# Score banks kept apart from query banks, and a planner that enters subtractions one by one

## What is computed

```python
xn = x / jnp.maximum(l2, 1e-12) * scale_norm * gamma
q, k, v = (qkv[:, :, 0], qkv[:, :, 1], qkv[:, :, 2])
sim = jnp.einsum('bihd,bjhd->bhij', q * scale_attn, k)
sim = jnp.where(causal_mask, neg, sim)
attn = jax.nn.softmax(sim, axis=-1)
out = jnp.einsum('bhij,bjhd->bihd', attn, v)
```

## Time and profile before

| | us |
|---|---|
| median of three runs | 1998.93 |
| the profiled execution, its own time | 2002.52 |
| its span in the profile | 2000.7 |
| big-head stage, from its first matmul to its last | 880.85 to about 1409.2 |

### The profile page before, as it was taken

One profiled execution on the slowest core, in us unless ns is written; L12 is line 12 of the kernel. 1 busy time (PEld: TensorE's weight loads), 2 busy tenths in 40 slices (PEclk: granted clock), 3 DMA queues, 4 the chain that ended last, 5 costly groups with the idle time before them and its releaser, 6 DMA issues. The chain is left out here.

```text
span 2000.7 us, 40527 instructions
## 1 busy us (share of the span) xinstructions
PE 1787.3 (89%) x15880; PEld 958.9 (48%) x15880; DVE 1559.0 (78%) x2275; ACT 1374.9 (69%) x2569; POOL 419.6 (21%) x650
## 2 busy tenths in 40 slices
PE   6799999999999888849999999899679999998785
PEld 2122222222222278826888888789312322233384
DVE  5899999999999443547988788877578979785434
ACT  3499999999999743426665666566347998888331
POOL 4201000000000403343432221312320011122413
PEclk8599999999999988969999999999868999999597
DMA  5000000000000168700000000000100000000274
GB/s 171 1 3 4 4 11 3 4 11 4 4 11 5 34 220 279 243 21 1 1 1 1 1 1 1 1 1 1 55 1 2 5 4 11 5 12 7 67 264 154
DMA packets 52878, 81.57 MB, mean 41 GB/s; under 512 B 9200, under 2 KB 37744, under 8 KB 52560
## 3 DMA queue, kind: packets, MB, share of 16 engines
q1 hardware_dynamic: 47520, 70.50, 11.1%
q0 software_dynamic: 3072, 6.30, 1.0%
q10 hardware_dynamic: 2096, 2.17, 0.4%
HBM read 64.13 MB, written 12.06 MB: 38 GB/s over the span
## 5 line engine op out<-in xcount | busy, mean ns | idle before, releaser
L827 DVE TENSOR_REDUCE a_mx<-psum 128x2 f32<-128x1024 f32 (+2 forms) x832 | 906.0, 1154 | 75.3 <-PE psum L602 42.2
L753 ACT ACTIVATE a_cs<-psum 128x512 f32<-128x512 f32 (+3 forms) x1664 | 856.9, 571 | 80.7 <-PE psum L620 62.5
L643 PE MATMUL psum<-a_cs,a_V 128*16 128x256 f32 (+1 forms) x6400 | 501.7, 384 | 20.8 <-ACT a_OD L733 9.7
L602 PE MATMUL psum<-a_KS,a_QS 48*128 48x512 bf16 (+3 forms) x1664 | 328.7, 386 | 30.4 <-DVE a_mx L827 27.3
L620 PE MATMUL psum<-a_QS,a_KS 51*128 51x512 bf16 (+3 forms) x1664 | 336.8, 379 | 4.9 <-ACT a_cs L753 3.0
L620 PEld LDWEIGHTS psum<-a_QS,a_KS 51*128 51x128 bf16 x1664 | 87.8, 93 | 354.9 <-ACT a_cs L753 310.1
L2159 PE MATMUL psum<-b_VW,b_ST 128*128 128x129 f32 x2176 | 249.4, 276 | 0.3 <-DVE X L2291 0.3
L2159 PEld LDWEIGHTS psum<-b_VW,b_ST 128*128 128x128 f32 x2176 | 245.4, 192 | 0.5 <-DVE X L2291 0.5
L643 PEld LDWEIGHTS psum<-a_cs,a_V 128*16 128x16 f32 x6400 | 107.1, 94 | 245.1 <-issue 120.5
L2266 DVE TENSOR_TENSOR b_M<-b_M,b_ST 128x512 f32<-128x512 f32 (+3 forms) x264 | 158.1, 599 | 40.5 <-ACT b_ST L2198 11.8
L2203 ACT ACTIVATE b_ST<-b_ST 128x2048 f32<-128x2048 f32 x48 | 91.8, 1911 | 124.6 <-DVE b_ST L2274 124.6
(11 more groups left out here) (233 smaller groups left out, 1773.7 us busy)
## 6 DMA issues: line engine op xcount, KB each, us to landing
e_W<-in_l_experts SPq DMA_DIRECT2D x45, 576.0 KB, 5.8
e_W<-in_l_experts SPq DMA_DIRECT2D x21, 768.0 KB, 5.7
yg<-e_yout SPq DMA_DIRECT2D x14, 256.0 KB, 6.0
xg<-zeros SPq DMA_DIRECT2D x2, 1472.0 KB, 9.7
a_cs<-in_rope ACTq DMA_DIRECT2D x4, 512.0 KB, 10.0
a_QS<-a_mrow SPq DMA_DIRECT2D x128, 3.0 KB
a_cs<-in_rope SPq DMA_DIRECT2D x1, 2048.0 KB, 7.7
a_num<-a_OD SPq DMA_DIRECT2D x120, 16.0 KB
```

The costliest lines, as they stand in the source:

```text
L602: mm = pe.matmul(ps[:, 2 * slot + half, 0:width], QS[rows, 2 * p + i, q_cols(qb, qt * P, P)], KS[rows, 2 * p + i, c * BLK:c * BLK + width] ...
L643: mm = pe.matmul(ps[32 * j:32 * j + 2 * HD, AV_BANK, a:b], V[:, kt, HPP * p + j, :], probs(e, a, b), start=(kt == 0 and half == 0), stop=last,
L753: act.activation(probs(HPP * s + j, c, BLK), ps[:, plan.bank(entry), c:BLK], ACT.Exp, scale=scale).then_inc(exp_done, 1)
L827: dve.tensor_reduce(mx[:, pk % 2, qt, 2 * i:2 * i + 2, c], banks, AX.X, ALU.max).then_inc(max_done, 1)
```

## The change

The ring is split. Score tiles get four banks (0 to 3), by their running number; bank 4 serves queries and transposes, one at a time; products keep banks 5 to 7. `subtract` becomes one event per group (`narrow`), dated 2.6 apart; wide exponentials are dated 3.8 behind their group's subtraction, and the diagonal's 1.5 behind its own, at the least 3.9 behind the last wide one. All of these sit in one sorted list, `timed`. The statistics of the layer norm become an event of their own (`stats`), dated 10, 12 and 14 behind the turn of atom 26; the power stays at the turn of atom 27. No instruction is added or taken away; only the order of the lists and the waits for banks differ.

```diff
     def turn(self):
         _, a = self.turns.pop(0)
         self.events.append(("reduce", a))
+        if a == NORM_ATOM - 1:
+            behind = max(n for n, (qb, h) in enumerate(self.atoms) if qb in EARLY_BLOCKS)
+            self.norms = [(self.clock + 10.0 + 2 * n, ("stats", g, behind)) for n, g in enumerate(EARLY_BLOCKS)]
         if a == NORM_ATOM:
-            behind = max(n for n, (qb, h) in enumerate(self.atoms) if qb in EARLY_BLOCKS)
             for n, g in enumerate(EARLY_BLOCKS):
-                self.norms += [(self.clock + 0.5 + n, ("measure", g, behind)), ...
+                self.norms += [(self.clock + 0.5 + n, ("measure", g)), ...
     def spread(self):
         _, a = self.spreads.pop(0)
-        self.events.append(("subtract", a))
         qb = self.atoms[a][0]
-        self.exps += [(self.clock + 1.5 + 2.3 * (g + 1), ("wide", a, g)) for g in range(qb)]
-        self.exps.append((self.clock + max(4.0, 1.5 + 2.3 * (qb + 1)), ("diagonal", a)))
+        for g in range(qb):
+            self.timed += [(self.clock + 2.6 * g, ("narrow", a, g)), (self.clock + 2.6 * g + 3.8, ("wide", a, g))]
+        behind = self.clock + 2.6 * qb
+        self.timed += [(behind, ("narrow", a, qb)), (max(behind + 1.5, self.clock + 2.6 * (qb - 1) + 3.9), ("diagonal", a))]
+        self.timed.sort()
...
-    RING, O_BANK, O_BANKS = 5, 5, 3
+    S_BANKS, G_BANK, O_BANK, O_BANKS = 4, 4, 5, 3
...
         def bank_of(event):
-            return plan.place_of[event] % RING
+            return (plan.tile0[event[1]] + event[2]) % S_BANKS if event[0] == "score" else G_BANK
         def wait_bank(eng, event):
+            if event[0] == "score":
+                n = plan.tile0[event[1]] + event[2]
+                if n >= S_BANKS:
+                    eng.wait_ge(copied, n - S_BANKS + 1)
                 return
-            what, of = plan.ring[n][:2]
+            n = plan.place_of[event]
+            if n == 0:
+                return
+            what, of = plan.single[n - 1]
             if what == "query":
                 eng.wait_ge(g_done, of + 1)
-            elif what == "fold":
+            else:
                 eng.wait_ge(norm.h_ready, early[of] + 1)
-            else:
-                eng.wait_ge(copied, plan.tile0[of] + plan.ring[n][2] + 1)
...
-                def subtract(a):
+                def subtract(a, g):
                     qb = plan.atoms[a][0]
-                    dve.wait_ge(row_done, a + 1)
-                    dve.wait_ge(max_done, plan.max0[a + 1])
-                    for g in range(qb):
+                    if g == 0:
+                        dve.wait_ge(row_done, a + 1)
+                        dve.wait_ge(max_done, plan.max0[a + 1])
+                    if g < qb:
                         ...
+                        return
                     for i in range(TPB):
                         ...
```

More of the change, by code:

```diff
@@ L1888, in __init__ @@
         self.events = []
-        self.clock, self.turns, self.spreads, self.norms, self.exps = 0.0, [], [], [], []
+        self.clock, self.turns, self.spreads, self.norms, self.timed = 0.0, [], [], [], []
         self.asked = 0
@@ L1910, in emit @@
             self.events.append(self.norms.pop(0)[1])
-        while self.exps and self.clock >= self.exps[0][0]:
-            self.events.append(self.exps.pop(0)[1])
+        self.due()
     def turn(self):
@@ L1916, in turn @@
         self.events.append(("reduce", a))
+        if a == NORM_ATOM - 1:
+            behind = max(n for n, (qb, h) in enumerate(self.atoms) if qb in EARLY_BLOCKS)
+            self.norms = [(self.clock + 10.0 + 2 * n, ("stats", g, behind)) for n, g in enumerate(EARLY_BLOCKS)]
         if a == NORM_ATOM:
-            behind = max(n for n, (qb, h) in enumerate(self.atoms) if qb in EARLY_BLOCKS)
             for n, g in enumerate(EARLY_BLOCKS):
-                self.norms += [(self.clock + 0.5 + n, ("measure", g, behind)), (self.clock + (12.0, 14.0, 47.0)[n], ("normalize", g)),
+                self.norms += [(self.clock + 0.5 + n, ("measure", g)), (self.clock + (12.0, 14.0, 47.0)[n], ("normalize", g)),
                                (self.clock + (45.0, 48.0, 54.0)[n], ("fold", g))]
@@ L1926, in spread, with due @@
         _, a = self.spreads.pop(0)
-        self.events.append(("subtract", a))
         qb = self.atoms[a][0]
-        self.exps += [(self.clock + 1.5 + 2.3 * (g + 1), ("wide", a, g)) for g in range(qb)]
-        self.exps.append((self.clock + max(4.0, 1.5 + 2.3 * (qb + 1)), ("diagonal", a)))
+        for g in range(qb):
[3 more added lines that the diff above has]
+        self.timed.sort()
+    def due(self):
+        while self.timed and self.clock >= self.timed[0][0]:
+            self.events.append(self.timed.pop(0)[1])
     def score(self, a):
@@ L1963, in lay @@
                 self.spread()
-            while self.exps and self.exps[0][1][1] <= a:
-                self.events.append(self.exps.pop(0)[1])
+            while any(event[1] <= a for _, event in self.timed):
+                self.events.append(self.timed.pop(0)[1])
             for half in range(2):
@@ L1968, in lay @@
                     self.emit(("product", a, kt, half), 0.265 * len(self.columns(a, kt, half)))
-        assert not self.norms and not self.exps
-        self.ring = [event for event in self.events if event[0] in ("query", "score", "fold")]
-        self.place_of = {event: n for n, event in enumerate(self.ring)}
+        assert not self.norms and not self.timed
+        self.single = [event for event in self.events if event[0] in ("query", "fold")]
+        self.place_of = {event: n for n, event in enumerate(self.single)}
 class HeadWeights:
@@ L2055, in bank_of @@
         def bank_of(event):
-            return plan.place_of[event] % RING
+            return (plan.tile0[event[1]] + event[2]) % S_BANKS if event[0] == "score" else G_BANK
         def wait_bank(eng, event):
-            n = plan.place_of[event] - RING
-            if n < 0:
+            if event[0] == "score":
+                n = plan.tile0[event[1]] + event[2]
+                if n >= S_BANKS:
+                    eng.wait_ge(copied, n - S_BANKS + 1)
                 return
-            what, of = plan.ring[n][:2]
+            n = plan.place_of[event]
+            if n == 0:
+                return
+            what, of = plan.single[n - 1]
             if what == "query":
                 eng.wait_ge(g_done, of + 1)
-            elif what == "fold":
+            else:
                 eng.wait_ge(norm.h_ready, early[of] + 1)
-            else:
-                eng.wait_ge(copied, plan.tile0[of] + plan.ring[n][2] + 1)
         def x_cols(g):
@@ L2304, in _ @@
                         maximum(event[1], event[2])
-                    elif event[0] == "subtract":
-                        subtract(event[1])
+                    elif event[0] == "narrow":
+                        subtract(event[1], event[2])
                     elif event[0] == "product" and event[2] == plan.last(event[1], event[3]):
                         accumulate(event[1], event[3])
-                    elif event[0] == "measure":
+                    elif event[0] == "stats":
                         dve.wait_ge(added, 2 * (event[2] + 1))
```

## The result

The changed kernel takes 2013.21 us (median of 4 runs, 2010.80 to 2018.29) against 2000.29 for the kernel before (4 runs): the ratio is 1.0064, 95% interval 1.0047 to 1.0080, so 12.9 us slower. The forecast was 2005.6, +6.7 us: the right side, and a little more than half of what came; the time lies 0.2 us outside the range.

A forecast was written before the change was run, and what follows sets the result against it. TensorE was nearly always busy, with a loop through VectorE and ScalarE nearly as long as its own work. Terms -3.0 + 6.5 - 0.9 + 1.9 + 0 + 2.1 and 0.1 gave +6.7: 2005.6 us, range 1994 to 2013.

The forecast's parts named there:

- small atoms: Atoms 0 to 15: GL comes earlier, so TensorE's waits at queries nearly go; -3.0 us, bounds 0 and -5.5.
- middle: Atoms 16 and 17: the wait for GL turns into one for a copy two tiles later; +0.1 us.
- qb 2: Atoms 18 to 23, main term: all twelve copies start behind the diagonal exponentials; +6.5 us, bounds 3.4 and 8.7.
- qb 3 and end: First atom of qb 3 -0.9, the three atoms from 25 to 28 +1.9, end of the stage +2.1 us.
- The loop: qb 2, subtraction through exponentials, copies, maxima and reduction to the next subtraction: from 18.41 to 19.56 us, +1.15 an atom.
- 5.0 + 3.75 + 10.81: qb 2: subtraction to GH, GH to the copies' start, first copy to next subtraction; together 19.56 us.
- 3.12 wait: First atom of qb 3: this wait for GL goes, and a 2.4 us wait at the ninth tile replaces it; net -0.9.
- the 6.11: TensorE's wait at the atom with the statistics: becomes 3.6 + 2.4 us with statistics one atom earlier.
- Atoms 28 to 31: 0: Late qb 3: GH no longer waits for TensorE, which pays for the accumulation; 0 us.
- Half of it: Rival: the query is not late, the qb 2 loop grows only 0.57 an atom; +2.5, 2001.4 us; chance 0.30.
- The waits go: Rival: TensorE sets the pace, all 19.7 us of waits for GL and 1.8 of clock vanish; 1977 us; chance 0.12.
- The clock falls: Rival: some 13 new waits of 1.5 to 3.6 us each cost 1.8 of clock, 23 on top; 2029 us; chance 0.08.

The follow-up runs named there:

- e2: The changed kernel with the old ring of five banks, so only the planner differs from the kernel before; 2010.98 us, 1.0042 of the kernel before.
- e1: The kernel before with only the new banks (four for scores, one for queries and transposes), old dates kept; 1998.62 us, 0.9983 of the kernel before.
- e4: The changed kernel with the statistics back at the turn of atom 27; 2012.19 us, 1.0047 of the kernel before.
- e5: The changed kernel with all pieces of a subtraction dated at one moment, exponentials as changed; 2006.47 us, 1.0019 of the kernel before.
- d1: c2 with half of the additions to the residual left out in the first sixteen atoms, so less VectorE work; 1993.01 us, 0.9949 of the kernel before.
- e3: The changed kernel with the diagonal exponentials dated as in the kernel before; 2004.65 us, 1.0010 of the kernel before.
- c3: c2 with the diagonal exponentials of qb 0 and 1 dated as in the kernel before; 1998.22 us, 0.9981 of the kernel before.
- c2: The changed kernel with the diagonal exponentials of qb 2 and 3 dated 16 behind the subtraction; 1998.41 us, 0.9981 of the kernel before.

## Why the prediction was right and wrong

By stretch, the terms of the sum against the stage (us):

| step | forecast | measured |
|---|---|---|
| value phase, 0–4 | not in the sum (0) | +3.4 |
| small atoms, 4–16 | -3.0 | -4.7 |
| middle, 16–19 | +0.1 | +4.2 |
| qb 2, 19–25 | +6.5 | +6.4 |
| qb 3 and end, 25–end (-0.9, +1.9, +2.1) | +3.1 | +2.3 |
| sum | +6.7 | +11.6 |

*qb 2, right in size and cause.* The loop was forecast at 19.56 and the wait at 1.8; the rows have 19.65 and 1.76, and its three parts, 5.0 + 3.75 + 10.81, are 5.03 + 3.74 + 10.88. The step's two causes show singly: the diagonal block ahead of the copies (+0.57 an atom forecast, +0.5 in e2) and the fifth tile tied to the first copy, which the four banks bring. That e1 alone pays 3.1 us, with the old dates, the step did not say.

*qb 3, near in the sum, not in its parts.* The 3.12 wait became 2.20 (forecast 2.4), the 6.11 became 3.10 and 1.98 (forecast 3.6 and 2.4), and the accumulation stands where it was put. The move of the statistics, priced within +1.9, is nothing by e4. "Atoms 28 to 31: 0" is wrong in its parts: waits of 1.27 to 1.52 stand there, and e5 puts the single entries at some 3.6 us from query 25 on. That the sum comes near is in part luck: from query 25 to the end the banks alone gain 3.0 us (e1) and the new dates alone lose 4.7 (e2). The forecast also counted a lowered clock only behind the 3.12; the kernel before has 0.83 over 1290 to 1310, behind the 6.11, and the changed one 0.91 over 1278 to 1298, which is some 3.4 and 1.8 us.

*Small atoms, the step that failed.* "At best TensorE gets ahead by its slack" was there, and the -3.0 was still booked as a gain. TensorE did get ahead, by 4.7, but the engine behind which it works was VectorE, busy 57.6 of 63 us, whose work did not shrink, and the head start came back as one wait of 2.22 and a lower clock behind it. Net over both stretches -0.5 instead of -2.9. That VectorE is what it waits for is seen in d1.

*Value phase, the step that was missing.* The forecast followed "diagonal behind wide" for qb 2 and 3 and left out the first atoms, where the same date puts the diagonal exponentials ahead of copies of the values: +3.4, back to 47.0 in e3 and c3. In the stage the two misses, 2.4 and 3.4, are the whole difference, less 0.9 of smaller errors of the other sign.

*The rivals.* "Half of it" is out: qb 2 paid 6.4, not 3.4. "The waits go" is out: GL's waits went, the copies' came. "The clock falls" is out for most of the waits that it counted: with six waits of 1.76 the stretch of qb 2 shows a granted clock of 1.00. It held behind the 3.10 us wait, for some 1.8 us, and at two places that it did not name, for about 1.5 and 1.6 us; over the whole stage the granted clock is 0.98 before and after.

The rule of the Trainium skill that was weighed (TensorE: Matmul & The Clock Gate, section "A second HAM failure mode: psum-queue depth-cycling") was that brief idling through PSUM banks keeps lowering the clock. In qb 2 of the changed kernel TensorE idles 1.76 us for a bank in each atom, and there the trace doesn't agree: 1.00.

What stays open: the median rose by 12.9 and the stage by 11.6; the 1.3 between them is smaller than the spread of single runs, and nothing was tried on it. Open too are the clock behind c3's 1.60 us wait, and whether VectorE's amount of work or the length of one accumulation paces the small atoms.

## What to carry to other kernels

On an engine that works off one list, an early entry isn't free because its input is ready: look at what stands behind it and who waits for that; here eviction copies that free PSUM banks belonged ahead of exponentials that nothing needed yet. When the engine that one frees isn't the one that sets the pace of a stretch, book its head start at zero and look for the place where it is waited off. And when a date is changed for all cases, go through every phase in which it falls due, the first two as well.

## What was not expected of the hardware

How long TensorE idled did not by itself say whether its clock fell. Six waits of 1.76 us, 19.65 apart, left the granted clock at 1.00, and so did the wait of 2.20 at 1233.04 (1.00 over 1233 to 1243). Waits of 0.77 and 1.36 us within 3 us in the value phase go with 0.93 over 905 to 930, six value matmuls taking 4.54 instead of 3.04; one of 2.22 us at 1042.53 goes with 0.91 over 1032 to 1052, thirty products taking 5.26 instead of 3.62; the same wait of 1.60 us goes with 0.79 in c2 and 0.57 in c3 over the 8 us around it. A slow stretch is from the slower of the two levels, 1.2 GHz in place of 2.4, for part of its time; what tells the places where it fell from those where it did not, no run here shows.
